# Three edits between the last four stages: a narrower second search, a looped general part of the first, and no clearing of semaphores

## What is computed

```python
def _quant_act_int8(x):
    amax = jnp.maximum(jnp.quantile(jnp.abs(x), 1.0 - 0.005), 1e-5)
    s = 127 / amax
    return jnp.clip(jnp.round(x * s), -128, 127) / s
def _quant_w_ternary(w):
    gamma = jnp.mean(jnp.abs(w)) + 1e-5
    return jnp.clip(jnp.round(w / gamma), -1.0, 1.0) * gamma
...
h = _layernorm(_layernorm(x), ln_g, ln_b)                    # 4096 x 512
h = _quant_act_int8(h) @ _quant_w_ternary(w1).T              # 4096 x 2048
h = gelu(h)
out = _quant_act_int8(h) @ _quant_w_ternary(w2).T
x = x + jnp.tanh(g_ffn[1]) * out
```

## Time and profile before

| what | us |
|---|---|
| median of 3 runs | 1367.39 (1365.78 to 1371.28) |
| the profiled execution | 1367.96 |
| its span in the trace | 1365.8 |
| PE busy | 1181.4 (86%) |
| DVE busy | 909.5 (67%) |
| ACT busy | 664.8 (49%) |
| first search, quantile1 | about 1052 to 1077 |
| product_tops | 1083 to 1211 |
| second search, quantile2 | 1212 to 1244 |
| ffn | 1245 to 1366 |

### The profile page before, as it was taken

One profiled execution on the slowest core, in us unless ns is written; L12 is line 12 of the kernel. 1 busy time (PEld: TensorE's weight loads), 2 busy tenths in 40 slices (PEclk: granted clock), 3 DMA queues, 4 the chain that ended last, 5 costly groups with the idle time before them and its releaser, 6 DMA issues. The chain is left out here.

```text
span 1365.8 us, 25075 instructions
## 1 busy us (share of the span) xinstructions
PE 1181.4 (86%) x9030; PEld 874.1 (64%) x9030; DVE 909.5 (67%) x2166; ACT 664.8 (49%) x1120; POOL 521.6 (38%) x448
## 2 busy tenths in 40 slices
PE   5899999999999997469999974999992299935998
PEld 4788888888888885357666622565561288932443
DVE  5667677677777765334444342799995699886874
ACT  3343344444434343113344341566774289657992
POOL 1233333333333432228767741366664000002442
PEclk9999999999999998689999996999996599966999
DMA  6223223322222221495788898999942689734994
GB/s 228 79 71 111 100 101 109 114 94 93 93 93 93 94 78 60 166 378 185 288 280 311 280 357 293 367 328 331 333 145 61 122 214 403 318 157 174 419 366 150
DMA packets 127616, 274.25 MB, mean 201 GB/s; under 512 B 44160, under 2 KB 55328, under 8 KB 120864
## 3 DMA queue, kind: packets, MB, share of 16 engines
q1 hardware_dynamic: 113856, 235.14, 48.2%
q0 software_dynamic: 10688, 36.71, 8.0%
q10 hardware_dynamic: 2976, 1.14, 0.3%
HBM read 155.26 MB, written 109.31 MB: 194 GB/s over the span
## 5 line engine op out<-in xcount | busy, mean ns | idle before, releaser
L1939 PE MATMUL p_z<-qT,w1T 128*128 128x256 bf16 (+1 forms) x1152 | 114.1, 262 | 14.5 <-DMA qT<-p_q 14.4
L970 PEld LDWEIGHTS p_sel<-p_pick,p_xp 128*128 128x128 bf16 x1536 | 91.1, 101 | 49.5 <-issue 40.3
L1939 PEld LDWEIGHTS p_z<-qT,w1T 128*128 128x128 bf16 x1152 | 102.5, 98 | 25.9 <-DMA qT<-p_q 14.5
L970 PE MATMUL p_sel<-p_pick,p_xp 128*128 128x128 bf16 x1536 | 102.5, 226 | 15.9 <-DMA p_xp<-xparts 15.0
L2404 POOL DMA_DIRECT2D p_y<-residual x32 | 27.0, 845 | 230.7 <-POOLq L113 198.6
L1117 DVE COPY p_selT<-p_sel 128x512 f32<-128x512 f32 x64 | 44.3, 692 | 102.5 <-PE p_sel L970 102.5
L2425 PE MATMUL p_o<-w2T,p_Gq 128*128 128x512 bf16 x384 | 86.6, 386 | 6.0 <-DVE p_Gq L2472 6.0
L618 POOL TENSOR_TENSOR p_rs<-p_ve,p_mhalf 128x2 f32<-128x2 f32 x32 | 22.3, 698 | 153.5 <-DVE p_ve L684 153.4
L1061 ACT ACTIVATE p_selT<-p_sel 128x512 f32<-128x512 f32 x64 | 38.2, 597 | 83.7 <-PE p_sel L970 83.7
L361 PE MATMUL p_M<-p_ctxTh,p_Wkh 128*128 128x256 f32 x256 | 75.4, 295 | 1.9 <-DVE p_Wkl L694 1.9
L361 PE MATMUL p_M<-p_xnTh,p_Wqh 128*128 128x256 f32 x256 | 75.0, 293 | 1.1 <-DVE p_V L767 1.1
(11 more groups left out here) (377 smaller groups left out, 3414.1 us busy)
## 6 DMA issues: line engine op xcount, KB each, us to landing
inter_d<-p_stage SPq DMA_DIRECT2D x64, 512.0 KB, 4.3
p_rows<-inter_d SPq DMA_DIRECT2D x32, 1024.0 KB, 9.4
activations<-hid SPq DMA_DIRECT2D x20, 1024.0 KB, 7.0
p_cin<-in_ctx_dram SPq DMA_DIRECT2D x32, 512.0 KB, 5.9
xparts<-p_parts SPq DMA_DIRECT2D x16, 768.0 KB, 3.2
activations<-third SPq DMA_DIRECT2D x12, 1024.0 KB, 6.7
hid<-activations SPq DMA_DIRECT2D x12, 1024.0 KB, 14.4
p_xp<-xparts SPq DMA_DIRECT2D x3, 3072.0 KB, 25.7
```

What stands on the lines that cost most here:

```text
L970: mm = pe.matmul(bsel[u % 2][:, k * P:(k + 1) * P], xp[:, c, tile, r, :], pick[sb % 2][:, tile, :, :].rearrange("p s g -> p (s g)"), start ...
L1939: mm = pe.matmul(bank, w1T[:, c, fc * P:(fc + 1) * P], qT[:, bass.ds(first, tiles), c, :], start=(c == 0), stop=(c == C - 1))
```

## The change

SPREAD becomes 64, so the bracket, `grid` and the table it is read from have 64 entries and quantile2 has 6 rounds. In the general part of quantile1 the 16 pairs of tiles are run over by a loop on DVE, with a semaphore of its own (`slow_pass`). The last four stages don't clear their semaphores at their ends: they keep them in `kept`, with numbers of their own (29 + 26 + 8 + 61 = 124), and one clear and one barrier stand at the end of the kernel; each stage's end has the block's barrier and one more. The other lines of the diff only pass `kept` to the four stages.

```diff
@@ -104,16 +104,28 @@
 @contextmanager
-def semaphores(nc, prefix, names):
+def semaphores(nc, prefix, names, kept=None):
     sems = {n: nc.alloc_semaphore(prefix + n) for n in names}
     yield sems
     nc.all_engine_barrier()
+    if kept is not None:
+        kept.extend(sems.values())
+        return
     nc.clear_and_free_semaphores(list(sems.values()))
     nc.all_engine_barrier()
 
-SPREAD = 256
+@contextmanager
+def kept_semaphores(nc):
+    kept = []
+    yield kept
+    nc.clear_and_free_semaphores(kept)
+    nc.all_engine_barrier()
+
+SPREAD = 64
@@ -1896,30 +1908,34 @@
             with dve.If(again > 0):
                 m = Count(dve, slow.s["aside"])
                 own = slow.s["own"]
-                pairs = TILES // 2
-
-                def magnitudes(k):
-                    v = hid[:, 2 * k:2 * k + 2, :]
-                    dve.scalar_tensor_tensor(junk[:, :].rearrange("p (t d) -> p t d", t=2), v, -1.0, v, ALU.mult, ALU.max).then_inc(own, 1)
-                    dve.wait_ge(own, m.next(own))
+                pairs, passed = TILES // 2, sw["slow_pass"]
+
+                def magnitudes(k, at):
+                    v = hid[:, bass.ds(k * 2, 2), :]
+                    dve.scalar_tensor_tensor(junk[:, :].rearrange("p (t d) -> p t d", t=2), v, -1.0, v, ALU.mult, ALU.max).then_inc(passed, 1)
+                    dve.wait_ge(passed, at + 1)
 
                 def count_all(i, trial, op):
-                    for k in range(pairs):
-                        magnitudes(k)
-                        dve.tensor_scalar(junk[:, :], junk[:, :], trial, 0.0, op, ALU.add, accum_out=parts[:, k:k + 1]).then_inc(own, 1)
-                        dve.wait_ge(own, m.next(own))
+                    m.apart()
+                    with dve.Fori(0, pairs) as k:
+                        at = i * (2 * pairs) + k * 2
+                        magnitudes(k, at)
+                        dve.tensor_scalar(junk[:, :], junk[:, :], trial, 0.0, op, ALU.add, accum_out=parts[:, bass.ds(k, 1)]).then_inc(passed, 1)
+                        dve.wait_ge(passed, at + 2)
                     dve.tensor_reduce(slow.cnt[:, :], parts[:, :], AX.X, ALU.add).then_inc(slow.s["asked"], 1)
...
```

More of the change, by code:

```diff
@@ L1720, in finish, with quantile1 @@
         dve.wait_ge(own, n.next(own))
-def quantile1(nc, cand, hid, K, amax, minus_t, tern_d, w1T, w2T):
+def quantile1(nc, cand, hid, K, amax, minus_t, tern_d, w1T, w2T, kept):
     rank, rank_above, low, high = quantile_ranks(N1)
@@ new lines, in least_of_all @@
+                    with dve.Fori(0, pairs) as k:
+                        at = k * 4 + (BITS + 1) * 2 * pairs
+                        magnitudes(k, at)
+                        dve.tensor_scalar(junk2[:, :], junk[:, :], found, 3e38, ALU.is_le, ALU.mult).then_inc(passed, 1)
+                        dve.wait_ge(passed, at + 2)
+                        dve.tensor_tensor(junk[:, :], junk[:, :], junk2[:, :], ALU.max).then_inc(passed, 1)
+                        dve.wait_ge(passed, at + 3)
+                        dve.tensor_reduce(parts[:, bass.ds(k, 1)], junk[:, :], AX.X, ALU.min).then_inc(passed, 1)
+                        dve.wait_ge(passed, at + 4)
@@ L1954, with product_tops @@
 GRID_GROUP = BASE_TILE + 2
-def product_tops(nc, hid, qT, w1T, gam, amax, zs, Gs, g_d, cand, K, base, grid):
+def product_tops(nc, hid, qT, w1T, gam, amax, zs, Gs, g_d, cand, K, base, grid, kept):
     rank_here = quantile_ranks(N2)[0] / (NB * P)
@@ L2134, in _, with quantile2 @@
                     dve.tensor_scalar(grid[:, :], grid[:, :], base[:, :], None, ALU.add).then_inc(s["base_done"], 1)
-def quantile2(nc, cand, K, zs, cut, small, amax, base, grid):
+def quantile2(nc, cand, K, zs, cut, small, amax, base, grid, kept):
     rank, _, low, high = quantile_ranks(N2)
@@ L2144, in quantile2 @@
         sbt = lambda n, sh, d=F32: es.enter_context(nc.sbuf_tensor("q2_" + n, sh, d))
-        s = es.enter_context(semaphores(nc, "qb_", "consts at_ready signed counted told own found gelu_done".split()))
+        s = es.enter_context(semaphores(nc, "qb_", "consts at_ready signed counted told own found gelu_done".split(), kept))
         junk, junk_a = sbt("junk", [P, NC2 - NA], BF16), sbt("junk_a", [P, NA], BF16)
@@ L2324, in __getitem__, with ffn @@
         return self.w[p, c, bass.ds(self.first, P)]
-def ffn(nc, Gs, spare, perm, g_d, w2T, gam, amax, gf, x3_d, out_d, cut, small, flag, rows, qT, w1T, zs, K):
+def ffn(nc, Gs, spare, perm, g_d, w2T, gam, amax, gf, x3_d, out_d, cut, small, flag, rows, qT, w1T, zs, K, kept):
     rank, prefix = quantile_ranks(N2)[0], "p8_"
@@ L2348, in ffn @@
         names += ["flag_done"] + [f"r_{n}" for n in "found in x q o done out".split()] + [f"q2s_{n}" for n in Search.NAMES + ["z_full", "gelu_done", "counted", "step_own"]]
[L2349 removed]
+        s = es.enter_context(semaphores(nc, prefix, names, kept))
         ov = out_d.rearrange("b (t p) d -> p (b t) d", p=P)
@@ L2502, in _, with feed_forward @@
             again(dve, redo.on_vector)
-def feed_forward(nc, es, room, spare, qT, w1T, w2T, gam, amax1, gf, K, x3_d, g_d, out_d, perm):
+def feed_forward(nc, es, room, spare, qT, w1T, w2T, gam, amax1, gf, K, x3_d, g_d, out_d, perm, kept):
     sbt = lambda n, s, d=F32: es.enter_context(nc.sbuf_tensor(n, s, d))
@@ L2512, in feed_forward @@
         base, grid = [e2.enter_context(nc.sbuf_tensor(n, [P, k], F32)) for n, k in (("base", 1), ("grid", SPREAD))]
-        product_tops(nc, room, qT, w1T, gam, amax1, zs, Gs, g_d, cand, K, base, grid)
-        quantile2(nc, cand, K, zs, cut, small, amax2, base, grid)
-    ffn(nc, Gs, spare, perm, g_d, w2T, gam, amax2, gf, x3_d, out_d, cut, small, flag, room, qT, w1T, zs, K)
+        product_tops(nc, room, qT, w1T, gam, amax1, zs, Gs, g_d, cand, K, base, grid, kept)
+        quantile2(nc, cand, K, zs, cut, small, amax2, base, grid, kept)
+    ffn(nc, Gs, spare, perm, g_d, w2T, gam, amax2, gf, x3_d, out_d, cut, small, flag, room, qT, w1T, zs, K, kept)
 def mk_flamingo_gated(nc, x, ctx, mask, gx, gf, Wq, bq, Wk, bk, Wv, bv, Wo, bo, ctrl, f1, f2, bias, ln_g, ln_b, w1, w2,
@@ L2538, in mk_flamingo_gated @@
         phase2b3(nc, inter_d, perm, gmask, gf, x_one, ctx, mask, gx, ln_g, ln_b, K, x_three, hid, cand, minus_t)
+        kept = es.enter_context(kept_semaphores(nc))
         amax1 = sbt("amax1", [P, 1])
         w1T, w2T = sbt("w1T", [P, C, DF], BF16), sbt("w2T", [P, FC, D], BF16)
-        quantile1(nc, cand, hid, K, amax1, minus_t, tern_d, w1T, w2T)
+        quantile1(nc, cand, hid, K, amax1, minus_t, tern_d, w1T, w2T, kept)
         qT = sbt("qT", [P, TILES, C, P], BF16)
-        feed_forward(nc, es, hid, cand, qT, w1T, w2T, gam, amax1, gf, K, x_three, g_d, out, perm)
+        feed_forward(nc, es, hid, cand, qT, w1T, w2T, gam, amax1, gf, K, x_three, g_d, out, perm, kept)
 _INS = ["x", "ctx_1024", "mask_Bx1xS2_fk0", "g_xattn", "g_ffn", "L0_xattn_Wq", "L0_xattn_bq", "L0_xattn_Wk", "L0_xattn_bk",
```

4 lines of the change are left out of this document (2 added, 2 removed).

## The result

| | before | after |
|---|---|---|
| median, us | 1368.11 (1365.78 to 1371.28, 4 runs) | 1354.23 (1353.05 to 1354.89, 4 runs) |
| the profiled execution, us | 1367.96 | 1353.92 |
| its span, us | 1365.8 | 1351.8 |

The ratio is 0.9898, 95% interval 0.9883 to 0.9913: 13.9 us less (11.9 to 16.0), where 13.15 were forecast. It is faster by more than 0.5%, all of the interval. The agreement is better than the working deserves, as the stages show. One of 17 executions of the kernel before that were timed beside e5 to e8 took 3,924.65 us for no known cause, and is left out of their ratios.

The account below looks back on a forecast made before the run. TensorE (PE) was busiest at 86%, but both searches and the wait after the first were taken as pure latency. From 1367.39 us, -7.7 - 4.8 - 0.6 - 0.4 + 0.35 = -13.15 gave 1354.2 us, range 1351 to 1360.

Parts of the forecast that it names:

- Part 1: Second search, quantile2: a bracket of 64 takes 6 rounds instead of 8, saving 7.7 us.
- The grid's smaller operations: In product_tops: a shorter DVE addition, Gelu and load save between nothing and 0.35 us; taken as 0.
- Part 2 with part 3 at the end of quantile1: End of quantile1: looped unexecuted code shortens DVE's jump, and clear and second barrier go; together 4.8 us saved.
- the jump costs 0.3 us, the row that is nearest in length: End of quantile1: DVE's branch to drain falls from 3.0 to 0.3 us, like the jump over Redo.
- the pause before L111 goes: End of quantile1: DVE's extra 1.8 us before that barrier's release, blamed on a block boundary, falls to 0.
- The inference from the packets: End of quantile1: instruction packets falling into DVE's two pauses, 3.0 and 1.8 us, mean that code is being fetched.
- rival (a): End of quantile1: the pauses at the jump stay, looping brings nothing, 1358.7 us; chance 0.16, in whole or part.
- Part 3: No clearing between stages: 0.6 us saved after product_tops, 0.4 after quantile2; one larger clear at the end adds 0.35.
- The clock: PE's half-clock time after restarts in product_tops and ffn, 2.9 and 4.8 us: no change taken, 1 us either way.
- The sum: Whole kernel: all savings and the longer final clear give 13.15 us less, a median of 1354.2 us.
- (b): Second search: the bracket misses the wanted integer and Redo runs in ffn, over 5,300 us; chance 0.03.
- (c): product_tops and ffn: PE's stretches grow through a later clock rise, about 1355.2 us; chance 0.80 together with the forecast.

Follow-up runs that it names:

- e5: The changed kernel with 100 small instructions added inside the first search's If, which isn't entered; 1357.47 us, ratio 0.9926.
- e8: The changed kernel without the barrier of L111 at the ends of the last four stages; 1353.55 us, ratio 0.9896.
- e9: The changed kernel with SPREAD = 32, a bracket of 32; 1350.51 us, ratio 0.9873.
- e10: The changed kernel with PE products nobody reads, in product_tops, quantile2 and ffn; 1348.59 us, ratio 0.9864.
- e1: The kernel before with only SPREAD changed from 256 to 64; 1359.24 us, ratio 0.9938.
- e4: The changed kernel with the general part of quantile1 written out as before; 1357.53 us, ratio 0.9926.
- e6: The changed kernel with 56 small instructions added inside the first search's If, which isn't entered; 1353.57 us, ratio 0.9900.
- e11: The changed kernel with PE products nobody reads and without the barrier of L111 at the last four stage ends; 1350.78 us, ratio 0.9882.
- e3: The kernel before with only the kept semaphores, not cleared between the last four stages; 1366.07 us, ratio 0.9990.
- e7: The kernel before with 12 very small DVE instructions added ahead of the jump in quantile1; 1367.21 us, ratio 0.9999.
- e2: The kernel before with only the general part of quantile1 looped; 1363.38 us, ratio 0.9969.

## Why the prediction was right, and where it wasn't

**Part 1** (-7.7): -7.64 alone, -7.31 in after. The term was right; what it lacked is 0.35 us in one round, which comes with the place of the code (it is there in after, e9 and e10, and in none of e1, e4, e5, e6, e8 and e11, where the code lies elsewhere).

**The grid's smaller operations** (0): the spread of tops with the clock's delay hides anything of that size. Taken at 0, not shown.

**Part 2 with part 3 at the end of quantile1** (-4.8): -4.49. Its own rows give 1083.34 - 1078.6 = 4.74, rounded up. The step "the jump costs 0.3 us, the row that is nearest in length" failed by 0.3: it is 0.6 in every kernel with the looped code. Length doesn't set this difference: the jump over Redo at the end of ffn, whose code is the same everywhere, takes 0.23 us in before, e1, e3, e5 and e7 and 0.56 in after, e2, e4, e6 and e8. The 0.33 between them is near the 0.35 us of the third round above; that both are a step into a new block fits, but isn't shown. The step "the pause before L111 goes" held. The inference from the packets, which rival (a) doubted, is supported from two sides: longer unexecuted code brings the first pause back (e5), 12 places of shift take the second away (e7). The Trainium skill ("Runtime: NRT & Kernel Launch", Instruction fetch mechanics) has the kind of rule; its page of 256 instructions would have left a jump of 182 within a window of two pages at most places, and e5 pauses for 3.0 us; here the measurement decides.

**Part 3** (-0.6, -0.4, +0.35): gap 2 gave -0.43. The 0.6 after product_tops lies within "tops": e3 shows -0.42 there with 0.3 us more of low clock, which is worth 0.15. The clear at the end took 0.698 us as worked out, 0.33 more than ffn's alone; the tail grew by 0.43, the rest being POOL's drain just before the clear (0.23 us in place of 0.14). DVE's drain also came 0.6 us behind its branch (1349.3 and 1349.9), 0.3 later than in the earlier trace rows, but this costs nothing: SP drains last in both kernels, 1.82 us behind the start of L2501 and L2517, and in e3, where DVE's drain isn't late, the tail is as long (3.59).

**The clock** (0, with 1 us either way): tops +0.75, ffn -0.55 in the profiled execution. Over the kernels the low time ran from 2.9 to 5.3 us in product_tops and from 3.1 to 5.6 in ffn. Of two kernels of this table without clears, e3 and e5, the one with 2.1 us more of low clock takes 1.12 us longer in tops: half, as assumed. The upper bound of 4.8 us was too low.

**The sum**: by its own steps the forecast was 1 us too high (13.15 against 12.2), of which 0.4 is the second search, 0.3 the jump, 0.1 the tail and the rest the clock. What filled the gap in the profiled execution is 1.9 us of scatter in stages that didn't change. The median of four runs isn't free of such scatter either, and the kernel before came out at 1368.11 in place of the 1367.39 that the forecast started from, so an agreement of 0.03 us between forecast and median says nothing about the working; that each stage agrees within 0.8 us does. One reading was loose: the chain from 1248.07 back to the barrier at 1244.86 has seven DVE instructions, not six short ones, and two of them last 1.30 and 1.24 us; nothing of the sum hangs on it.

**Rivals**: (a) fell. (b) had only a lower bound for its price, too low by nearly five times for a chunk; its place holds: a bracket that misses makes the kernel fifteen times slower, and the distance left is 16 integers. (c) was real in product_tops and made up for in ffn.

## What to carry to other kernels

Code that is never entered isn't free: a jump over it waited when its target was 182 instructions ahead or more and not at 138 or less, here 3 us on the path, and a rolled loop in the untaken branch takes that away. What the loop costs when the branch is taken wasn't measured. Before counting on a few tenths from barriers or a shorter chain, look at what PE's clock does behind it, since a restart's delay alone moved two stages by over a microsecond each. A narrower search pays by whole rounds, but its price is that of the fallback times the chance to need it: work out where the answer lies in the bracket before narrowing it.

## What the runs showed of the hardware that I had not expected

DVE's unexecuted code is paid for at the jump: 2.9 to 3.1 us for jumps of 182 and 271 instructions, 0.6 us for 82 and 138. 12 more executed instructions took away a pause of 1.8 us. A step of DVE into a new block may cost 0.35 us in the middle of a chain even when it comes in sequence (seen in three kernels with the same DVE code up to there, and gone in six others; no instruction was shifted for this alone). The granted clock stays at 1.2 GHz for 2.9 to 5.6 us after PE starts again, and 14 unread products in an idle stretch take that out of the next stage.
